# Unread turnings on TensorE at four pauses of a four-layer kernel

## What is computed

```python
x = x + attn_a(layernorm(x))   # differential attention, 16 heads of 8, causal, two softmax maps
x = x + ffn(layernorm(x))      # 8 experts, top 2: silu(x@wg) * (x@wu) @ wd, weighted and summed
x = x + attn_b(layernorm(x))   # 16 heads of 64: S = a*S + k v^T, out = q.S / (q.z + eps), then @ Wo
x = x + ffn(layernorm(x))      # the same experts again
```

## Time and profile before

| | us |
|---|---|
| median of 3 runs | 1133.96 (1132.32 to 1134.56) |
| the profiled execution, its own time | 1133.05 |
| span of the profiled execution | 1131.3 |
| PE busy in it | 1004.9 (89%) |
| DVE busy | 749.7 (66%) |
| ACT busy | 749.2 (66%) |
| mean granted clock of TensorE | 0.942 of 2.4 GHz |

### The profile page before, as it was taken

One profiled execution on the slowest core, in us unless ns is written; L12 is line 12 of the kernel. 1 busy time (PEld: TensorE's weight loads), 2 busy tenths in 40 slices (PEclk: granted clock), 3 DMA queues, 4 the chain that ended last, 5 costly groups with the idle time before them and its releaser, 6 DMA issues. The chain is left out here.

```text
span 1131.3 us, 26078 instructions
## 1 busy us (share of the span) xinstructions
PE 1004.9 (89%) x9820; PEld 689.8 (61%) x9820; DVE 749.7 (66%) x1513; ACT 749.2 (66%) x1513; POOL 437.5 (39%) x580
## 2 busy tenths in 40 slices
PE   5889999999999999749999489999999999489993
PEld 3333333333333334538999457787888888479993
DVE  6699999999999997882333445656565656443333
ACT  4658888887888887445665666575766665356663
POOL 3752112211122211227674034544444444256761
PEclk9889999999999999968999588999999999679997
DMA  2243111111111100611112311120212120021114
GB/s 71 84 124 103 31 31 49 39 31 30 31 46 43 31 2 3 223 38 50 48 48 55 135 70 76 39 76 39 76 39 76 39 75 2 10 61 48 50 41 126
DMA packets 40033, 64.65 MB, mean 57 GB/s; under 512 B 10024, under 2 KB 21032, under 8 KB 37992
## 3 DMA queue, kind: packets, MB, share of 16 engines
q1 hardware_dynamic: 31736, 50.14, 14.0%
q0 software_dynamic: 4992, 10.23, 3.4%
q10 hardware_dynamic: 3184, 2.63, 0.7%
HBM read 47.86 MB, written 14.68 MB: 55 GB/s over the span
## 5 line engine op out<-in xcount | busy, mean ns | idle before, releaser
L802 ACT ACTIVATE PB<-S 128x512 f32<-128x512 f32 x576 | 307.9, 597 | 71.0 <-PE S L608 66.1
L908 DVE TENSOR_REDUCE mx<-S 128x2 f32<-128x1024 f32 (+1 forms) x192 | 207.5, 1127 | 7.6 <-PE S L594 7.6
L870 POOL TENSOR_SCALAR_AFFINE_SELECT PB<-PB 128x512 f32<-128x512 f32 x128 | 79.0, 635 | 306.6 <-ACT PB L802 306.5
L643 PE MATMUL PV<-PB,VP 128*32 128x256 f32 (+2 forms) x2432 | 177.7, 379 | 0.0
L1503 DVE TENSOR_TENSOR m_hs<-m_gs,m_UP 128x512 f32<-128x512 f32 x78 | 53.6, 688 | 159.4 <-ACT m_gs L1348 157.2
L608 PE MATMUL S<-W 50*128 50x512 bf16 (+3 forms) x768 | 123.9, 328 | 4.9 <-ACT PB L802 4.2
L594 PE MATMUL S<-W 48*128 48x512 bf16 (+3 forms) x640 | 94.3, 326 | 13.1 <-DVE mx L904 4.9
L1202 POOL DMA_INDIRECT yd_rows<-m_ys,m_target x78 | 76.6, 982 | 59.9 <-DVE m_ys L1510 59.9
L1196 POOL DMA_INDIRECT m_xs<-xn_rows,m_source x78 | 75.8, 972 | 48.0 <-DVE m_source L1483 24.8
L643 PEld LDWEIGHTS PV<-PB,VP 128*32 128x32 f32 x2432 | 51.6, 108 | 69.2 <-issue 59.4
L594 PEld LDWEIGHTS S<-W 48*128 48x128 bf16 x640 | 26.8, 94 | 107.9 <-issue 43.9
(11 more groups left out here) (311 smaller groups left out, 1948.8 us busy)
## 6 DMA issues: line engine op xcount, KB each, us to landing
d_LQ<-l_rows SPq DMA_DIRECT2D x15, 1024.0 KB, 4.6
W<-qk_parts SPq DMA_DIRECT2D x210, 32.0 KB
qk_parts<-OT SPq DMA_DIRECT2D x24, 256.0 KB, 3.1
W<-qk_parts SPq DMA_DIRECT2D x30, 96.0 KB
W<-in_L_ffn_w_gate SPq DMA_DIRECT2D x1, 2048.0 KB, 9.8
W<-in_L_ffn_w_up SPq DMA_DIRECT2D x1, 2048.0 KB, 14.8
xn_rows<-m_XN SPq DMA_DIRECT2D x8, 256.0 KB, 2.3
m_GB<-yd_rows SPq DMA_DIRECT2D x8, 256.0 KB, 5.6
```

Of the source, the lines that this page charges most:

```text
L643: ins = nc.tensor.matmul(PV[32 * u:32 * u + 32, shift + col:shift + end], VP[:, g, kb, u // 2, :], PB[:, slot, col:end], start=(kb == 0 an ...
L802: nc.scalar.activation(PB[:, j % NPB, :], S2[:, j % 3, :], ACT.Exp, scale=SC).then_inc(exp_done, 1)
L870: nc.gpsimd.affine_select(out=tri, in_=tri, compare_op=ALU.is_ge, fill=0.0, base=0, pattern=[[0, U], [1, P]], channel_multiplier=-1).then_ ...
L908: nc.vector.reduce_max(mx[:, g % 2, c, :, heads[0], qb], S1[:, b, :, 0:w], AX.X)\
```

## The change

Turnings whose result nobody reads are added on PE at four places, and the turning of the normalised rows is written so that each row waits for itself.

- Prologue: six turnings of `XN` into `tp`, after PE's last product and before the change of blocks.
- First maxima: four turnings of `ident` into `PV` after each slot from number `N1` on, among the slots ahead of the main loop (eight slots, so 32 turnings).
- Combine: 26 turnings into `UP[:, 1]` after `output_weights`, two after each of the 16 waits for `weighted`, one between the rows of a quarter, four after each of the first three quarters, eight at the end. `rows_turn` waits for each row by itself instead of for the whole quarter.
- Decay: after `step(0, 0)` PE waits for `supd_done` of 1 and runs ten turnings into `SU`.

```diff
--- before.py
+++ after.py
@@ -266,6 +266,9 @@
                                                 stop=True)
                     last.then_inc(lx_done, 1)
 
+                    for _ in range(6):
+                        nc.tensor.transpose(tp[:, 0, 0:P], XN[:, 0, :], ident[:])
+
                 @block.scalar
                 def _(act):
                     with nc.allow_non_contiguous_dma("router weights, 4 KiB"):
@@ -714,6 +717,10 @@
                         while n < N1 and u < units_upto[n]:
                             unit(u)
                             u += 1
+
+                        if n >= N1:
+                            for _ in range(4):
+                                nc.tensor.transpose(PV[:, 0:P], ident[:], ident[:])
                     pe.wait_ge(values_taken, N0)
                     pe.wait_ge(dve_rest, len(by_dve))
                     pe.wait_ge(p0_ready, len(items))
@@ -1294,15 +1301,22 @@
                                                     route["RWC"][:], start=True, stop=True)
                     last.then_inc(wor_done, 1)
 
+
+                def unread_products(count):
+                    for _ in range(count):
+                        nc.tensor.transpose(UP[:, 1, 0:P], ident[:], ident[:])
+
                 def rows_turn(q):
-                    if q < NQ - 1:
-                        pe.wait_ge(rows_ready, TQ * q + TQ)
-                    else:
-                        pe.wait_ge(last_rows, TQ)
                     if q >= 2:
                         pe.wait_ge(turned_copied, q - 1)
                     for j in range(TQ):
+                        if q < NQ - 1:
+                            pe.wait_ge(rows_ready, TQ * q + j + 1)
+                        else:
+                            pe.wait_ge(last_rows, j + 1)
                         last = nc.tensor.transpose(GP[:, q % 2, j * P:(j + 1) * P], XN[:, TQ * q + j, :], ident[:])
+                        if j < TQ - 1:
+                            unread_products(1)
                     last.then_inc(rows_turned, 1)
 
                 def decay_logits(q):
@@ -1317,11 +1331,18 @@
 
                 if follow is not None:
                     output_weights()
+                    unread_products(26)
+                    for t in range(NT):
+                        pe.wait_ge(weighted, t + 1)
+                        unread_products(2)
                     for q in range(NQ):
                         rows_turn(q)
                         if q:
                             decay_logits(q - 1)
+                        if q < NQ - 1:
+                            unread_products(4)
                     decay_logits(NQ - 1)
+                    unread_products(8)
 
             @block.scalar
             def _(act):
@@ -1851,6 +1872,10 @@
                 scores(0, 0, 0)
                 pe.wait_ge(e_ready, 4)
                 step(0, 0)
+
+                pe.wait_ge(supd_done, 1)
+                for _ in range(10):
+                    nc.tensor.transpose(SU[:, 0:P], ident[:], ident[:])
                 step(1, 1)
                 over_pairs(pe, 2, NT - 1, step)
                 step(NT - 1, (NT - 1) % 2, last=True)
```

## The result

The median of the change is 1129.75 us (11 runs, 1122.77 to 1134.62) against 1133.96 us for the kernel before on the same chip (11 runs, 1131.86 to 1135.42); the ratio is 0.996, 95% interval 0.9942 to 0.9978. That is faster by some 4.5 us, between 2.5 and 6.6. The forecast was 6.4 us faster. The profiled execution of the change took 1128.02 us, 5.0 less than the profiled one of before.

The account below looks back on a forecast made before the run. At half clock PE bounds after the change of blocks and in the decay, DVE the maxima, a DMA-DVE-ACT-PE chain the combine. 0 - 0.8 - 2.5 - 3.1 = -6.4 from 1133.05 gives 1126.6 us; range 1121.8 to 1131.5.

Parts of the forecast that it names:

- prologue: Before the change of blocks: six turnings hidden behind POOL, too few and too late to hold the clock; 0.
- first maxima: Slots ahead of the main loop: 32 turnings hidden under DVE, clock stays, DVE's waits for slow PE shrink; -0.8 us.
- combine: After `output_weights`: turnings keep full clock, so the last 16 products end at 648.9 instead of 651.4; -2.5 us.
- decay: After the first decay step: ten turnings fill PE's 1.23 us wait, second step's stretch falls from 7.24 to 4.11; -3.1 us.
- the third rival: Maxima and decay: the clock's fall only moves, the combine's gain alone stays; 1130.5 us, chance 0.10.
- The first rival: Prologue: its six turnings hold the clock too, 3.8 us more gained; 1122.8 us, chance 0.25.
- Rival 2: Combine: turnings too thin to hold the clock, about +1 instead of -2.5 us; 1130.1 us, chance 0.13.
- the bound of 1.6: Combine's slow end: at half clock 55 instructions of 0.21 us run without a break to 652.8 or later; +1.6 us.
- Rival 4: All places: turnings do not keep the clock and cost time, +1.6 combine, +0.9 decay, +0.3 maxima; 1135.9 us, chance 0.07.

Follow-up runs that it names:

- the denser version: the ends too, with two turnings instead of one between a quarter's rows and seven instead of four after it: 1125.87 us, ratio 0.9936.
- the routing too: the denser version plus turnings in both routings of the expert layers: 1126.76 us, ratio 0.9936 to the kernel before.
- five places: Kernel before plus turnings in prologue, combine (seven, seven, four after quarters; 14 at end), decay start, first step and end; none in maxima: 1128.3 us, ratio 0.9945.
- the ends too: Change without prologue and maxima turnings; 14 after the combine, 4 at decay start, 9 after its first step, 12, 4, 5 at its end: 1125.56 us, ratio 0.9925.
- the thin turnings: Kernel with the combine's turnings alone, each made 8 rows by 8 columns, same number, place and order: 1136.65 us, ratio 1.0026.

## Why the prediction was right, and which term was wrong

The forecast, 1126.6 for the profiled execution or 1127.5 for the median, was right on the side, and its range held the time; 1129.75 is 2.3 us above. Part of the nearness is luck: in the two profiles the places that the forecast names give 3.7 us up to step 15, with the loss at the head in it, and another 1.4 us come at places that it does not name. By the steps of the prediction:

| term | forecast | alone, median of runs | what the profiles show |
|---|---|---|---|
| prologue | 0 | -1.5 (-2.7 to -0.2) | the clock falls in all four kernels with it, at 33.5 to 35.0; no gain at the head |
| first maxima | -0.8 | +2.5 (+1.5 to +3.5) | fall moves to 81.3 and 82.2, held in one |
| combine | -2.5 | -5.1 (-7.6 to -2.6) | -2.26 at DVE's wait; +0.95 behind `keys` |
| decay | -3.1 | -4.6 (-6.1 to -3.2) | -3.13 |
| combine and decay | -5.6 | -6.6 (-8.6 to -4.6) | |
| all | -6.4 | -4.5 (-6.6 to -2.5) | -3.7 at step 15, -5.1 at the last expert product |

**Decay, right in kind and size.** The turnings are hidden, the wait of 0.65 does no harm, and 7.24 becomes 4.11 as the third step had shown. Seven profiles with turnings there show 4.11 or 4.12. Without them five show 7.18 to 7.29, and two 5.62 and 5.63: there the clock was low for 3.4 us only.

**Combine, right at its end, short behind it.** "Then 16 instructions at full clock": 1.92 us, DVE's wait 2.54 where I had said some 2.3. "The next late thing is DVE's sums, then the change of blocks, which keep their length" holds so far, 2.93 us from the sums to `keys` in both. What it left out is the block behind, to which the forecast gave "a few tenths" of gain or nothing. In the execution before the clock was low until 658.3 and `keys` began at 654.36, so 3.9 us of the new block ran at half clock. Now `keys` began at 652.86, but the clock, fallen in PE's wait of 2.05 us for POOL, was low until 659.0: 6.1 us. Half of the 2.2 us more is 1.1; measured is 0.95, from 13.03 to 13.98. In the three profiles in which the 14 and 4 turnings held the clock there (the denser version, the routing too, five places) it is 12.35 or 12.36, and from the sums to that `OX` 15.45 or 15.46: that low stretch was the cost.

**First maxima, the step that failed.** "With them PE is at work some 0.8 of every 1.15 us there, and I expect the clock to stay." It stayed as long as there were turnings, and for 4.6 us more. But the last of them ends at 77.57, and the waits of DVE that were to be gained lay between 80 and 85.2, in the main loop, where none stand; there the clock fell, at 82.2. That is the mechanism of the third rival, "the fall only moves", at this place alone; in the decay it did not occur. I had counted only the low clock that goes and not the one that comes, and the latter stands where DVE bounds less. The size of the loss rests on the runs of two kernels (1.0012 and 1.0022). Its place is only partly shown: from the first exponential to that of group 1 the profile of before has 23.93 us, the change 24.09, prologue and maxima 25.46, the maxima alone 22.84.

**Prologue, right.** Too little and too late: the clock fell in each of the four profiles with the six turnings, and they delayed nothing. They end at 34.05, while POOL's last work there, line 215, ends at 34.22, and from PE's last product to its first work behind the change of blocks it is 1.89 us as before. The first rival is out by these profiles; the -0.13% of the six turnings' own runs is not explained by anything at the prologue.

**Rival 2, the combine does not hold**, is true of some executions: of the five profiles with one turning between the rows (the change, combine and decay, combine alone, the ends too, five places) three have a fall in the quarters, and the one at 646.0 costs 1.4 us, near the bound of 1.6. So a forecast of one value hid a mixture. The runs of the change span 11.9 us, those of before 3.6; that this rival makes the spread fits, with 4.0 and 4.6 us in the two kernels with two turnings between the rows, but it is not shown, and the five runs of the last kernel span 1.2.

**Rival 4, turnings useless**, is out. From 631.80 to 652.10 the clock was 1.00 with 114 instructions, 80 of them turnings. The sentence of the Trainium skill that full clock "doesn't engage for transpose-mode" ("TensorE: Matmul & The Clock Gate", Part 4) does not agree with that stretch. Its mechanism exists, though, and is dearer than I had it: where the stream does not hold the clock, as with the thin turnings, the combine costs 7.71 - 4.80 = 2.9 us (my bound was 1.6; where the rest arises I did not follow), and this place alone makes the kernel 0.26% slower.

The parts do not seem to add: -0.45% and -0.41% alone, -0.58% together, though intervals this wide (0.13 to 0.22 to either side) could make the 0.28. In the profile of the combine alone the decay's stretch is 5.63 us and the decay's end 21.03, both better than before with nothing done to them. The same two figures, 5.62 and 21.03, stand in the profile of the prologue alone. The moments at which the clock falls far behind the added turnings differ from profile to profile, and part of a kernel's gain or loss comes from that. I take this as the likeliest reason for the missing sum; it is not shown for the medians, nor that the turnings move those moments.

## What to carry to other kernels

Fill a pause of TensorE where TensorE bounds what follows, with full 128x128 work, ahead of a wait that it must stand through anyway; and see that the fill reaches as far as the waits that it is to shorten. Then read the stretch behind the filled one too, since a low clock that has only moved costs by what it meets there. Never let unread work stand between a late input and the product that waits for it: at half clock it takes twice the time just where none is to spare. A gain by the clock is a gain in some executions more than in others, so judge it by the median of many runs, never by one profile.

## What the runs showed of the hardware

- A busy PE is not enough for full clock. It was 0.50 through 34.1 us with turnings of 8 rows by 8 columns, PE busy 27.86 and, from 637.9 to 651.5, 13.59 of 13.60; 1.00 through 20.3 us with turnings of 128 by 128, PE busy 16.68. Nor do full turnings always bring it back: it stayed 0.50 for 13.5 us with PE busy 13.50, in full turnings and products of 24 columns (the ends too).
- The clock can fall without a long pause: in the change at 82.17, with PE busy 3.07 us from 77.60 to 82.10 and no pause above 0.51.
- A turning of 128x128 fp32 takes 0.13 us in a row of ten (1.31), 0.16 in a batch of four (0.66), and 0.20 at half clock (24 in 4.69).
- Executions of the same instructions have their low stretches at different places. The profiled execution of the change had one at 54.9 to 58.3 that before had not, ahead of any turning that could have moved it but the prologue's; five of the kernels tried had one there, three of them without these six (the thin turnings 54.2, the ends too 55.5, the routing too 55.4), and those three are the kernel before up to there. In the runs of the change itself the mean granted clock goes from 0.950 to 0.966, and the longest runs, 1134.45 and 1134.62 us, have the lowest.
